# GpSimd or VectorE for the normalised tokens of three layernorms

## The reference

```
_layernorm(x): (x - mean(x)) / sqrt(var(x) + 1e-5)
x = x + attention(_layernorm(x))        # 16 heads of 8, decay, softmax
x = x + experts(_layernorm(x))          # 160 experts, top 8, and a shared one
x = x + memory(_layernorm(x))           # 16 chunks of 64 tokens, a 128x128 state each step
x = x + experts2(_layernorm(x))         # 8 experts, grouped top 2
```

## Time and profile before

| | us |
|---|---|
| median of 3 runs | 1117.31 (1117.04 to 1119.65) |
| the profiled execution | 1117.76 |
| its span in the profile | 1115.8 |
| norm 1, first x complete to last tile transposed | 350.7 to 362.4 |
| norm 2, the same | 837.9 to 849.1 |
| norm 3, the same | 934.9 to 947.2 |

### The profile page before, as it was taken

One profiled execution on the slowest core, in us unless ns is written; L12 is line 12 of the kernel. 1 busy time (PEld: TensorE's weight loads), 2 busy tenths in 40 slices (PEclk: granted clock), 3 DMA queues, 4 the chain that ended last, 5 costly groups with the idle time before them and its releaser, 6 DMA issues.

```text
span 1115.8 us, 20193 instructions
## 1 busy us (share of the span) xinstructions
PE 1039.4 (93%) x5244; PEld 688.9 (62%) x5244; DVE 831.3 (75%) x1965; ACT 804.8 (72%) x1310; POOL 222.3 (20%) x326
## 2 busy tenths in 40 slices
PE   5899999999996589999999999999998998799997
PEld 3222222232325278888888888888876777587785
DVE  8544444343345779999999999999986887598897
ACT  6599999999992468787878787877774443266664
POOL 3767664444442000000000000000004112000000
PEclk9799999999997899999999999999999998799999
DMA  4368776666661176666666666666621000123321
GB/s 142 116 213 259 221 235 204 208 208 216 210 211 42 36 301 238 235 244 244 240 249 239 239 237 235 240 248 245 239 79 41 1 1 1 59 99 117 111 86 38
DMA packets 91894, 190.43 MB, mean 171 GB/s; under 512 B 10700, under 2 KB 55372, under 8 KB 81612
## 3 DMA queue, kind: packets, MB, share of 16 engines
q1 hardware_dynamic: 91860, 190.05, 49.9%
HBM read 154.03 MB, written 35.98 MB: 170 GB/s over the span
## 4 chain that ended last, share of the span: by engine, by line
PE 82%; DVE 8%; ACT 4%; issue 3%; DMA 2%; POOL 2%; ACTq 0%; DVEq 0%; SPq 0%; POOLq 0%
PE bank L1259 26%; PE bank L1272 15%; PE bank L1129 10%; PE bank L1266 8%; PE bank L1111 6%; PE bank L1114 6%; ACT ring L897 2%; PE bank L1361 2%; PE bank L1140 1%; POOL m_norm L786 1%; PE bank L1345 1%; DVE xn L1452 1%; DMA ring<-c_rows 1%; DVE stats L1440 1%; PE bank L1077 1%
## 5 line engine op out<-in xcount | busy, mean ns | idle before, releaser
L897 ACT ACTIVATE ring<-bank,minus_bound 128x1024 f32<-128x1024 f32 x256 | 271.4, 1111 | 22.9 <-DVE bank L1553 11.9
L1259 PE MATMUL bank<-xh,w_parts 128*128 128x512 f32 x896 | 277.2, 391 | 1.9 <-DVEq L1679 1.9
L958 ACT ACTIVATE bank<-bank 128x512 f32<-128x512 f32 x320 | 186.2, 582 | 90.8 <-PE bank L1259 90.8
L1693 DVE TENSOR_TENSOR bank<-bank,ring 128x512 f32<-128x512 f32 x320 | 223.9, 700 | 29.7 <-DMA ring<-c_rows 6.8
L1272 PE MATMUL bank<-hh,w_parts 128*128 128x512 f32 x776 | 239.7, 390 | 0.0
L1685 DVE TENSOR_TENSOR hl<-bank,hh 128x512 fp32r<-128x512 f32 x321 | 218.6, 681 | 0.1
L1553 DVE TENSOR_TENSOR bank<-bank,corner 128x128 f32<-128x128 f32 x256 | 76.6, 299 | 170.4 <-PE bank L1114 170.2
L952 ACT ACTIVATE hh<-bank 128x512 fp32r<-128x512 f32 x321 | 190.4, 593 | 3.2 <-DVE bank L1693 3.1
L1259 PEld LDWEIGHTS bank<-xh,w_parts 128*128 128x128 f32 x896 | 167.9, 188 | 38.0 <-DVEq L1679 2.3
L1259 PE MATMUL bank<-xl,w_parts 128*128 128x512 f32 x448 | 174.7, 390 | 0.0
L1272 PEld LDWEIGHTS bank<-hh,w_parts 128*128 128x128 f32 x776 | 145.9, 188 | 30.6 <-ACT hh L952 0.4
(11 more groups left out here) (281 smaller groups left out, 1135.4 us busy)
## 6 DMA issues: line engine op xcount, KB each, us to landing
ring<-c_rows SPq DMA_DIRECT2D x80, 1024.0 KB, 5.0
w_parts<-w_pairs SPq DMA_DIRECT2D x160, 128.0 KB, 2.5
w_pairs<-xh SPq DMA_DIRECT2D x16, 768.0 KB, 4.4
q_stack<-q_parts SPq DMA_DIRECT2D x64, 144.0 KB
k_stack<-k_parts SPq DMA_DIRECT2D x192, 48.0 KB
w_pairs<-xl SPq DMA_DIRECT2D x16, 512.0 KB, 2.9
ring<-c_rows SPq DMA_DIRECT2D x16, 512.0 KB, 4.6
big<-in_w_exp SPq DMA_DIRECT2D x16, 384.0 KB, 4.8
```

Source lines behind the costliest of these rows:

```text
L897: act.activation(ring[:, c % RING * S:(c % RING + 1) * S], wide[c % 2][:], ACT.Exp, bias=minus_bound[:]).then_inc(exp_done, 1)
L958: act.activation(bank(4 + c % ZB), bank(4 + c % ZB), ACT.Silu).then_inc(silu_ready, 1)
L1259: ins = pe.matmul(out_, w[i], x_[j], start=start and k == 0, stop=stop and k == 2, skip_group_check=not start)
L1693: dve.tensor_tensor(bank(4 + c % ZB), bank(4 + c % ZB), cb[u][:, g * GW:(g + 1) * GW], ALU.mult).then_inc(hid_ready, 1)
```

## The change

For k = 0 all stays. In norms 1 to 3 GpSimd, behind the power of a group, waits for it, issues the four `tensor_scalar` of that group itself and raises `xn_ready`; only then does it go to the next group. VectorE issues no L1452 in these norms. `rstd_ready` is raised in norm 0 alone.

```
                     pool.wait_ge(var_ready, G * k + g + 1)
                     link(pool.tensor_scalar(rstd[:, ts], mv[:, ts, 1], EPS, None, ALU.add))
-                    pool.tensor_tensor(rstd[:, ts], rstd[:, ts], half[:, ts], ALU.pow).then_inc(rstd_ready, 1)
+                    ins = pool.tensor_tensor(rstd[:, ts], rstd[:, ts], half[:, ts], ALU.pow)
+                    if k == 0:
+                        ins.then_inc(rstd_ready, 1)
+                    else:
+                        link(ins)
+                        for t in range(ts.start, ts.stop):
+                            ins = pool.tensor_scalar(xn[:, t, :], x[:, t, :], mv[:, t, 0:1], rstd[:, t:t + 1], ALU.subtract, ALU.mult)
+                            if t < ts.stop - 1:
+                                link.sign(ins)
+                        link.wait()
+                        ins.then_inc(xn_ready, 1)
...
-                    if g >= 1:
+                    if k == 0 and g >= 1:
                         tiles = range((g - 1) * TPG, g * TPG)
                         dve.wait_ge(rstd_ready, G * k + g)
```

## The result

The changed kernel takes 1149.52 us (median of 4 runs, 1147.68 to 1153.55) where the kernel before takes 1117.38 beside it: a ratio of 1.0295, 95% interval 1.0262 to 1.0327, so 32 us slower. The direction was forecast; the size was not: 8.4 us, with 1132.5 us as the upper end.

A forecast was written before the change was run, and what follows sets the result against it. VectorE was taken to set each norm's pace, 2.28 us a group, before TensorE's end; moved tokens make GpSimd a series. Norms 6.56 plus meetings 1.8 give 8.4 us over 1117.31: 1125.7 us, range 1119.5 to 1132.5.

The forecast's parts named there:

- price s: Time from the start of one GpSimd token instruction to the next, taken as 0.36 us, with bounds 0.23 and 0.45.
- The sum: Loss of the three norms without meetings, 48s - 10.72 = 6.56 us; with 1.8 for meetings, 8.4 us.
- The bound from above: Upper limit of a GpSimd token instruction, 0.45 us for 128 numbers, from subtractions at 2.16 ns a number.
- The bound from below: Lower limit of a GpSimd token instruction, 0.23 us for 128 numbers, from copies and casts at 0.83 ns a number.
- dear pointers: Rival: GpSimd's token instruction costs 0.55 us, giving 17.5 us more and 1134.8 us; chance 0.08.
- Norm 1: GpSimd's token series makes the last tokens later, so the last transposes start at 363.61 instead of 361.98: +1.63 us.
- Norm 3: GpSimd's token series makes the last transposes start at 947.77 instead of 946.20: +1.57 us.
- Norm 2: Inverse lengths queue behind 16 token instructions on GpSimd and delay the weighted sums: +3.36 us, called the largest term.
- Meetings: VectorE's rests xl meet GpSimd's tokens six times in norms 1 and 3, 0.3 us each: 1.8 us.
- Full lock: Rival: each VectorE rest holds GpSimd for its whole 0.68 us, 10.7 us in all, 1128.0 us; chance 0.18.
- The clock: Rival: TensorE's clock falls in norm 2, slowing the sums by 3.6 us, 12.0 in all, 1129.3 us; chance 0.12.
- norms 1 and 3 hide what is below s = 0.26: TensorE's own queue was the pace in both norms, so token instructions cheaper than 0.26 us cost nothing there.

The follow-up runs named there:

- the first execution: First profiled execution of the changed kernel, unaltered; its set of runs had a median of 1149.52 us, ratio 1.0295 to the kernel before.
- the changed kernel again: The changed kernel unaltered, in a second set of runs on another chip; ratio 1.0294 to the kernel before.
- e2: The changed kernel with the move in norm 2 alone, norms 1 and 3 as before; ratio 1.0097 to the kernel before, 10.8 us slower.
- e6: The changed kernel, but VectorE waits for the last tokens of norms 1 and 3 before its first rest xl; ratio 1.0255 to the kernel before.
- e7: The changed kernel with 13 more TensorE matmuls in norm 1 whose results nobody reads; ratio 1.0261 to the kernel before.
- e12: The changed kernel with VectorE's rests held until the last tokens and the 13 extra matmuls, both at once; ratio 1.0247 to the kernel before.
- e10: The changed kernel with GpSimd copying x to xn in place of each token instruction, arithmetic left out; ratio 1.0047 to the kernel before.
- e11: The changed kernel with each token instruction replaced by a GpSimd product with a tile of ones, arithmetic left out; ratio 1.0117 to the kernel before.
- e4: The changed kernel with a group's four token instructions made as two wide GpSimd instructions with spread operands; ratio 1.0163 to the kernel before.

## Why the prediction was wrong in size

The step that failed is the price s of the token instruction. I took 0.36, with 0.45 as the upper bound; it is 0.785. The sum multiplies it by 48, so this alone is 48 x 0.425 = 20.4 us of the 24 missing; the router's clock behind norm 1, a term that the sum did not have, is 3 more. The bound from above was no bound: it came from subtractions of two tiles on the idea that two inputs cost most. For a product of two tiles that reading was close (0.43), but `tensor_scalar` costs more there, 0.50 with a single constant. The bound from below, the copy, was right for a copy (0.25). The nearest row, 0.26 us for 8 numbers with two steps, was continued at the copy's 0.83 ns a number, where 3.4 applies: 0.26 + 120 x 3.4 ns = 0.67, and with the 0.16 of the pointers 0.83, a little over what was measured.

The rival "dear pointers" had the right direction with 0.55 and a chance of 0.08. By its own working, with 0.785, it gives 48 x 0.785 - 10.72 + 1.8 = 28.8 us; measured were 32 to 33. So the rest of the sum was nearly right:

- Norm 1: 16 x 0.785 - 4.13 = 8.4 and 1.1 for meetings, measured 9.5. Norm 3: 8.4 and 1.1, measured 9.45.
- Norm 2: 16 x 0.785 - 2.40 = 10.2, measured 10.0 in the first execution, where the inverse lengths were the last wait, as I had read. In the five other executions with these tokens in norm 2 (the changed kernel again, e2, e6, e7, e12) the stage took 26.3 us, 10.8 more than before, and the last wait was TensorE's queue of token scalars, a path that the sum did not hold. With the cheaper tokens of e10, e11 and e4 it was the inverse lengths. And norm 2 is not "the largest term" by much once s is large; that held near my s only.
- Meetings: 1.8 forecast, 2.2 measured. Full lock, the reading of the Trainium skill's rule ("SBUF — State Buffer", section "Who interferes with whom") in both directions, would be 4.1. GpSimd was held 0.51 or 0.08 us by rests of 0.69, and twice a norm it was the one held though it had begun first, so the trace agrees that the two hold each other up, and not that the whole instruction is paid or that the first to begin goes free.
- The clock: I looked for its fall in norm 2, and it did fall there. In the first execution (0.50 from 860 to 870) it cost nothing that shows, since TensorE waited for GpSimd anyway and was back at 1.00 when the sums came. In the five others it caught the token scalars ahead of the sums, 3.2 to 3.4 us instead of 1.81, and cost 0.8 us of the stage; the sums, which the rival had slow, took 3.64 as before. No run kept the clock up there, so what norm 2 would take without its fall is not shown. It cost 3 us in the router behind norm 1, which no rival named.
- Wrong, and without effect on the sign: "norms 1 and 3 hide what is below s = 0.26". Without tokens they became 2.8 and 3.5 us shorter. VectorE's tokens were the pace, as the row of 2.28 us a group had said; TensorE's queue kept back 1.4 of the 4.1 us that the sum gives norm 1 at s = 0.
- The statement of the Trainium skill ("GPSIMD Engine Reference", section "Engine selection") that one-input work runs on GpSimd at roughly line rate does not hold for this operation: 2.6 ns a number with one constant, against 0.83 for the copy.
- "Faster" at 0.02 and "slower" at 0.85 had the direction right; the upper end of the range lay 17 us too low.

## What to carry to other kernels

In these rows GpSimd's price goes by the operation, not by how much it reads: measure the very instruction, with its pointers and steps, in an idle stretch before a sum that multiplies it by 48. If pointers are needed there, two wide instructions with spread operands are cheaper than four with pointers. An engine that is 20% busy over a program may have 0.8 us of room in each 2.3 of the stage in question. A stage that makes TensorE wait can send its bill on to the next one, through the clock. And one profile shows one path: the last wait of norm 2 was another in the first execution than in the five after it.

## What was not expected of the hardware

- On GpSimd `tensor_scalar` on 128x128 costs 0.50 us with one constant, 0.62 with two, 0.785 with two pointers; a copy 0.25, a product of two tiles 0.43.
- A 128x512 `tensor_tensor` with one operand spread by a stride of nought took 1.04 us there, plain ones 1.16 to 1.28.
- After 20 us of waiting between short bursts the granted clock stayed at 0.50 for 10 us of the following stage; with 13 matmuls whose results nobody reads it was at 1.00 there, and the stage was 3 us shorter.
- A GpSimd token instruction that met a VectorE subtraction with two SBUF inputs of 0.69 us took 1.31 us instead of 0.79, though it had begun 0.1 us earlier; the subtraction kept its 0.69.
- The first 50 us of the same kernel had TensorE's squares at 7.0 or 10.0 us in different executions, and the medians did not tell the two apart.
